# Batch search of the second attention step: ten of sixteen halvings over 209 candidates in place of 1664; in the layer norm, three small copies moved later on VectorE

## What is computed

```
def _top_p_attention(X, W1, W2, W3):
    q = X @ W1.T @ W2.T
    k = X @ W3.T
    probs = softmax(q @ k.T, axis=-1)
    sp = probs sorted downwards in each row; cs = cumsum(sp)
    keep = cs - sp < 0.9                  # the largest entries that make up 0.9 of the row
    A = probs * keep
    return A / A.sum(-1)

def layer0(X, S):                         # for n in range(2):
    Xf = R @ Xf                           #   R: rows of S + I, divided by their sums
    Xa = _top_p_attention(Xa, W1, W2, W3) @ Xa
    Z = Z + Xf @ U1[n].T + Xa @ U2[n].T
    return layernorm(X + Z) * ln_g + ln_b

x = layernorm(x + layer0(x, adj))
x = layernorm(x + layer1(x, adj, adj))    # GRU cells and three graph attention heads
```

## Time and profile before

| | |
|---|---|
| time, median of 3 runs (lowest to highest) | 2703.39 us (2696.13 to 2705.26) |
| the profiled execution, its own time | 2697.63 us |
| its span | 2695.8 us |
| PE busy | 2329.1 us (86%) |
| DVE busy | 2159.1 us (80%) |
| ACT busy | 1069.1 us (40%) |
| POOL busy | 152.2 us (6%) |

### The profile page before, as it was taken

One profiled execution on the slowest core, in us unless ns is written; L12 is line 12 of the kernel. 1 busy time (PEld: TensorE's weight loads), 2 busy tenths in 40 slices (PEclk: granted clock), 3 DMA queues, 4 the chain that ended last, 5 costly groups with the idle time before them and its releaser, 6 DMA issues. The chain is left out here.

```text
span 2695.8 us, 53797 instructions
## 1 busy us (share of the span) xinstructions
PE 2329.1 (86%) x17795; PEld 1969.8 (73%) x17795; DVE 2159.1 (80%) x6687; ACT 1069.1 (40%) x1803; POOL 152.2 (6%) x342
## 2 busy tenths in 40 slices
PE   7999999879889978889967369987999999999985
PEld 2666666657777867767757368976999999999942
DVE  4777777578787888888889677758999999999836
ACT  5666666434334434334421220014444334443323
POOL 0000000101111110010000100000000000000000
PEclk8999999989999989999978779999999999999987
DMA  3000000022223312222202225551333433334220
GB/s 133 2 1 1 1 1 1 1 102 93 88 103 113 118 52 103 103 95 94 103 18 102 108 101 211 210 190 52 132 128 117 140 103 133 124 122 135 79 90 26
DMA packets 57310, 244.88 MB, mean 91 GB/s; under 512 B 6929, under 2 KB 18576, under 8 KB 43344
## 3 DMA queue, kind: packets, MB, share of 16 engines
q1 hardware_dynamic: 57040, 241.99, 25.7%
HBM read 235.15 MB, written 6.82 MB: 90 GB/s over the span
## 5 line engine op out<-in xcount | busy, mean ns | idle before, releaser
L2103 PE MATMUL a_acc<-H,pT 128*128 128x128 f32 x4056 | 547.8, 277 | 11.6 <-ACT a_rows L2135 3.8
L2103 PEld LDWEIGHTS a_acc<-H,pT 128*128 128x128 f32 x4056 | 495.3, 192 | 28.6 <-DVE pT L2237 19.9
L991 PE MATMUL small<-XR,wT 128*128 128x128 f32 x2756 | 378.2, 283 | 27.5 <-ACT wT L1261 26.8
L991 PEld LDWEIGHTS small<-XR,wT 128*128 128x128 f32 x2756 | 343.8, 197 | 43.3 <-ACT wT L1261 43.3
L862 PE MATMUL lg<-kT,qs 128*128 128x512 f32 (+1 forms) x742 | 339.1, 593 | 27.0 <-ACT e L1179 16.8
L72 DVE MAX8 cand<-e 128x8 f32<-128x64 f32 (+3 forms) x1898 | 302.9, 241 | 47.5 <-issue 24.6
L2237 DVE TENSOR_TENSOR pT<-a_tr,a_adjT 128x512 f32<-128x512 f32 (+1 forms) x546 | 316.7, 645 | 20.7 <-PE a_tr L2062 15.6
L2062 PE MATMUL a_tr<-ident,prob 128*128 128x128 f32 x2028 | 311.3, 274 | 10.9 <-ACTq L2129 10.9
L1261 ACT ACTIVATE wT<-tr 128x512 f32<-128x512 f32 (+1 forms) x371 | 206.3, 566 | 274.6 <-PE tr L981 273.6
L891 PE MATMUL accR<-XR,adj 128*128 128x129 f32 x2704 | 314.0, 276 | 0.0
L891 PEld LDWEIGHTS accR<-XR,adj 128*128 128x128 f32 x2704 | 309.9, 193 | 0.0
(11 more groups left out here) (351 smaller groups left out, 2423.8 us busy)
## 6 DMA issues: line engine op xcount, KB each, us to landing
adj<-in_adjT SPq DMA_DIRECT2D x52, 1664.0 KB, 7.2
g_adj<-in_adjT SPq DMA_DIRECT2D x26, 1664.0 KB, 7.0
a_adj<-in_adj SPq DMA_DIRECT2D x26, 1664.0 KB, 6.9
a_adjT<-in_adjT SPq DMA_DIRECT2D x156, 256.0 KB, 3.9
a_adjT<-in_adjT SPq DMA_DIRECT2D x26, 128.0 KB, 4.3
XT<-in_x_t SPq DMA_DIRECT2D x1, 1664.0 KB, 7.2
hT_scratch<-hT SPq DMA_DIRECT2D x1, 1664.0 KB, 11.1
nsT_scratch<-nsT SPq DMA_DIRECT2D x1, 1664.0 KB, 5.3
```

Source lines behind the costliest of these rows:

```text
L991: mm = eng.matmul(accA[:, :], wT[(k * NC + c - 1) % 2][:, o:o + P], xa[:, j, 0:P], start=(j == 0), stop=(j == T - 1))
L2103: mm = eng.matmul(acc[:, :], pT[g % RING][:, (j % 4) * P:(j % 4 + 1) * P], H[:, j, :], start=(j == 0), stop=(j == T - 1))
```

## The change

`solve_halving` has a new argument `wide`. At halving number `wide` (6 in the batch, never elsewhere) it calls `narrow`, which takes the upper end of the bracket (`mid` + `step`), leaves the candidates below it in `work` (one pass over 1664), takes the 8 largest of each 64 of them (26 MAX8: 208 values), puts the mass already found above the bracket behind them as the 209th candidate, and raises `tau` to the largest eighth value. The ten halvings left, and the passes L234, L239 and L257, then run over these 209. In the norm, the wait for the head vectors and their three copies stand behind the first norm's second half instead of ahead of its first.

```
+WIDE_HALVINGS = 6
-        self.round_cand = sb("round_cand", [P, -(-width // ROUND_SEG), 8])
+        n_round = -(-width // ROUND_SEG)
+        self.few_cand = sb("few_cand", [P, n_round * 8 + 1])
+        self.round_cand = self.few_cand[:, 0:n_round * 8].rearrange("p (a b) -> p a b", b=8)
...
+    def narrow(self, eng, cand, step, done):
+
+        mass, low = self.mass[:, 0:done, 0:1], self.low[:, 0:done, 0:1]
+        spare, rest = self.work[:, 0:cand.shape[1]], self.few_cand.shape[1] - 1
+        eng.tensor_tensor(low, mass, self.one("theta", 0).unsqueeze(1).to_broadcast([P, done, 1]), ALU.is_lt)
+        eng.tensor_scalar(self.round_mid[:, :], self.mid[:, 0:1], float(step), None, ALU.add)
+        eng.drain()
+        eng.scalar_tensor_tensor(spare, cand, self.round_mid[:, :].bitcast(F32), cand, ALU.is_lt, ALU.mult)
+        eng.tensor_tensor(low, mass, low, ALU.mult)
+        eng.drain()
+        segment_tops(eng, spare, cand.shape[1], self.round_cand, cand.shape[1] * 8 // rest)
+        eng.tensor_reduce(self.few_cand[:, rest:rest + 1], low.rearrange("p n k -> p k n"), AX.X, ALU.max)
+        eng.drain()
+        eng.tensor_reduce(self.one("best", 0), self.round_cand[:, :, 7], AX.X, ALU.max)
+        eng.drain()
+        eng.tensor_tensor(self.one("tau", 0), self.one("tau", 0), self.one("best", 0), ALU.max)
+        eng.drain()
+
+    def solve_halving(self, eng, cand, halvings, wide=None):
...
         for h in range(halvings):
+            if h == wide:
+                self.narrow(eng, cand[0], step, h)
+                cand = [self.few_cand[:, :]]
+                spare = [self.work[:, 0:cand[0].shape[1]]]
...
-                        find.solve_halving(eng, [find.fine[:, :, :].rearrange("p a b -> p (a b)")], FINE_HALVINGS)
+                        find.solve_halving(eng, [find.fine[:, :, :].rearrange("p a b -> p (a b)")], FINE_HALVINGS,
+                                           wide=WIDE_HALVINGS)
...
                     mean(half(i))
-                eng.wait_ge(v_summed, 1)
-                for part in range(3):
-                    copy = eng.tensor_copy(V[:, part, :], vp[:, :, part % 2])
-                copy.then_inc(v_ready, 1)
                 for i in range(2):
                     deviation(0, i)
...
                     mean(half(i))
+                eng.wait_ge(v_summed, 1)
+                for part in range(3):
+                    copy = eng.tensor_copy(V[:, part, :], vp[:, :, part % 2])
+                copy.then_inc(v_ready, 1)
                 clear_diagonal(0, 0)
```

More of the change, by code:

```diff
@@ L197, in solve_sorted @@
         self.end(eng, False)
-    def solve_halving(self, eng, cand, halvings):
+    def narrow(self, eng, cand, step, done):
[15 more added lines that the diff above has]
+    def solve_halving(self, eng, cand, halvings, wide=None):
         tiles, n = range(len(cand)), len(cand)
```

## The result

| | before | with the change |
|---|---|---|
| median of 7 runs (lowest to highest) | 2702.58 us (2696.13 to 2707.12) | 2692.51 us (2690.37 to 2696.97) |
| ratio to before, 95% interval | | 0.9965 (0.9953 to 0.9978) |
| profiled execution, span | 2695.8 us | 2693.0 us |
| DVE busy | 2159.1 us | 2143.9 us |

Faster by 0.35%, with an interval from 0.22% to 0.47%. The forecast was 0.23%, 2697.1 us, inside the range of 2690 to 2703. The forecast's 0.9977 lies in all three intervals. The three intervals overlap, so I take the first measurement's 10 us for a lucky one; no trace shows anything behind it. The forecast gave its largest share, 0.67, to a time within 0.3% of before: the first measurement lies just outside that, the two later ones (0.19%) inside.

What follows compares the result with a forecast made beforehand. DVE's batch search sets the end behind 1489 us, with PE's late rows running beside it ahead of that. Search -6.5, norm 0, copies +0.2 give -6.3 us: median 2703.39 becomes 2697.1 us, range 2690 to 2703.

Steps and rivals of the forecast that it cites:

- DVE's side of the search: Batch search on DVE: narrowing 6.4 us, ten halvings of 1.06, tail 8.4; flags at 1481.8 instead of 1495.8, 14.0 us sooner.
- PE's idle time as the cap: Ahead of L917: the search saves no more than PE's idle time there; 6.5 us saved, about 7.5 of DVE's gain lost waiting.
- The step that lets L917 run at 1489.42 and not at 1495.90: PE's flags' turn behind the late rows: ACT's copy at 1488.98 plus 0.44 handover, so 6.5 us saved.
- the clock: Rival: PE's half-speed stretches near 1510 and 1578 us fall otherwise, giving 2692 or 2702 us; chance 0.12 each way.
- The norm: Moving the head vectors' copies: 0 for removing DVE's 6.42 us wait, 0.2 us lost at their new place.
- The bound of 0.44 gained: Norm, taking the copies away ahead of L1871: the most it could gain, 0.44 us, around a forecast of 0.
- the bound of 0.3 lost: Norm: one DVE instruction gets in ahead of POOL's second add and delays that add by 0.34 us; 0.3 lost.
- POOL as the holder: Norm, L1871: its first instruction, 3.39 us, ends at 1545.33 because it waits for POOL's second add, ending at 1545.18.
- The rival in which the train of thirteen keeps the ports: Norm, L1871: DVE's instructions hold the ports ahead of POOL's second add, saving up to 3.05 us, 2694.0 us; chance 0.10.
- The extra round: Rival: narrow raises tau too far for one row, DVE runs another_round with PE idle; 38 us, 2735 us; chance 0.02.
- The sum: Whole kernel: -6.5 for the search, 0 for the norm's wait, +0.2 for the copies, -6.3 us together.

Runs made afterwards that it cites:

- the two later ones: The changed kernel, unaltered, measured twice more against the kernel before: 2695.57 us, ratio 0.9981, and 2696.74 us, ratio 0.9981.
- e5: The changed kernel with narrow's pass over 1664 candidates run three times more than needed, 6.1 us more DVE work; 2689.54 us, a single run.
- e4: The changed kernel with PE's flags' turn moved ahead of the last half unit of adjacency rows; 2685.25 us, 0.9939 of the kernel before.
- e7: The changed kernel with the copies at their old place and POOL's two adds left out; DVE's first sum to PE's first turn of H took 33.27 us.
- e9: The changed kernel with the narrowing after four halvings instead of six; 4746.31 us, a single run, 2045 us slower than before.

## Why the prediction was right, point by point

**DVE's side of the search**: right, 6.4 us for the narrowing, 1.06 for a halving, the flags 14.1 us sooner where 14.0 were forecast. Two shapes of the same instruction in one trace fixed the slope, and MAX8 in a train took 3.39 / 26 = 0.130 us against 0.128.

**PE's idle time as the cap**: right in kind (e5: six more microseconds on DVE cost nothing; e4: the gain comes back when the flags' turn leaves its place behind the late rows). Its size was the one term that was off. I read the last update's end, 1488.94, from one execution, the only one of the first six profiled in which the clock came back early at 1440. In the others the narrowed search gains 57.1 - 53.0 = 4.1 us, with the early clock 57.1 - 50.7 = 6.4. The step that lets L917 run at 1489.42 and not at 1495.90, with 6.5 us saved, holds for one of two cases, and for the rarer one (5 of 14 profiled executions). I had listed the clock as a rival, but at other places (1510 and 1578), not under the very time from which the cap was read.

**The norm**: 0 for the wait removed and 0.2 for the copies was forecast; together 0.06 was measured. The bound of 0.44 gained held (0.15). The case that came, one DVE instruction ahead of POOL's second add, stands in the prediction as the bound of 0.3 lost; it gained, because the add was put off by only 0.11 us and one instruction less was left to do behind it. POOL as the holder, argued then from 1545.33 against 1545.18, is now shown (e7). By the Trainium skill ("SBUF — State Buffer", the section on SBUF's two separate sides) the lock is taken for one instruction by whoever starts first. The traces with the change agree: one DVE instruction of 0.34 us goes first, POOL's add lasts 3.80 instead of 3.69, and the next DVE instruction waits 3.78. The rival in which the train of thirteen keeps the ports did not come; no run shows more than one instruction ahead of the add.

**The extra round**: it did not come with six halvings, and does with four, as the count on the inputs said. Its price of 38 us was the round alone; the whole event costs 2045 us. With a chance of 0.02 it would have belonged outside any range, but the rival as I wrote it was not the one that could have happened.

**The sum**: -6.3 us. With the term put right it is -4.1 or -6.4 by the clock, plus 0.06; weighted by 9 and 5 of 14 executions that is an estimate of 4.9 us. Three measurements gave ratios of 0.9965, 0.9981 and 0.9981, which are 9.5, 5.1 and 5.1 us. So the mechanism carried the forecast, while its size was read from the rarer case; the range had room for either (2699.3 with 4.1). What the first measurement has above them no trace explains.

## What to carry to other kernels

When one of two chains that run side by side is made shorter, price the gain by when the other is ready, and read that from several executions if a clock or a landing moves it. What is left on the shortened side is not lost: put the handover into the other engine's queue where it is ready, and the rest of the gain comes back (here 10 us for one moved call, more than the later measurements gave the change itself). And a long wait (here 6.42 us) may be worth nothing when the next instruction waits for another engine anyway; ask that next instruction first.

## What the runs showed of the hardware that I had not expected

The granted clock stayed low, and fell, with PE busy. With the change the head projection (52 matmuls with 9 columns out, each with its own weight load) kept PE busy all the time, and the clock stayed at 0.50:

```profile
1575.00:1578.50 3.50, 3.50 (x18) 3.50 (x18) 0.43 (x2) 0.00 (x0) 0.00 (x0) 0.50 0.00 0
1578.50:1584.50 6.00, 6.00 (x30) 6.00 (x29) 0.00 (x0) 0.00 (x0) 0.00 (x0) 0.50 0.00 0
```

In before the clock was up when these matmuls began (1575.65) and fell to 0.50 while they ran; the row ahead of the one in the earlier trace rows is:

```profile
1575.00:1578.50 3.50, 2.96 (x27) 2.86 (x26) 2.16 (x2) 0.59 (x2) 0.00 (x0) 0.98 0.02 5
```

Over the runs they take 8.15 to 11.27 us, which is as much scatter as the gain in question. And in e9 DVE stood 16.96 us without any wait in view at the first step behind the extra round, and mostly 2.4 us ahead of each turn of the loop; what it did in that time no view shows.
